# A new order for a hand-ordered two-layer transformer kernel, an earlier release of the routing banks, and ScalarE's Exp in the head attention

## What is computed

```python
xn = layernorm(x)                                    # layer 0
A  = tril(1 + s + s**2/2)                            # s = q.k/4 per head: 16 heads, feature size 16
y  = (A @ v) / rowsum(A) @ Wo.T
l  = sigmoid(xn @ gate_w) + gate_bias                # top 2 of 4 groups, then top 2 of 8 experts
f  = sum_top2 w * (silu(xn@w_gate[e]) * (xn@w_up[e])) @ w_down[e] + shared(xn)
x  = x + y + f

xn = layernorm(x)                                    # layer 1, over c (batch), t, h
p  = softmax_c((q[c,t,h] . k[c,t,h]) / sqrt(128))    # the "head attention": over the 4 batches
x1 = p[c,t,h] * sum_t v[c,t,h,:]
idx, score = top1(softmax(xn @ w_red @ norm(wg).T))
x2 = (gelu(xn @ w1[idx] + b1[idx]) @ w2[idx] + b2[idx]) * score
out = x + x1 + x2
```

## Time and profile before

| | before |
|---|---|
| median of 3 runs | 296.53 us (294.93 to 298.2) |
| the profiled execution's own time | 297.9 us |
| its span, first to last instruction | 296.2 us |
| PE busy | 261.4 us, 88% |
| DVE busy | 185.4 us, 63% |
| ACT busy | 140.2 us, 47% |
| POOL busy | 78.7 us, 27% |
| granted TensorE clock, mean | 0.954 |

### The profile page before, as it was taken

The page is one execution under the profiler, slowest core; times in us unless marked ns, Lnnn a source line. Parts: engine busy times, 40 slices in busy tenths (PEclk is TensorE's granted clock), DMA queues, the critical chain, the costliest instruction groups (busy, mean ns, idle before and its releaser), DMA issues.

```text
span 296.2 us, 6413 instructions
## 1 busy us (share of the span) xinstructions
PE 261.4 (88%) x2185; PEld 166.1 (56%) x2185; DVE 185.4 (63%) x523; ACT 140.2 (47%) x231; POOL 78.7 (27%) x113
## 2 busy tenths in 40 slices
PE   7879997899899988999999999999998719399990
PEld 5434642355553544765343945445687719299990
DVE  4759519966852477655178676768597699733330
ACT  1582724755546145434652536562633415246660
POOL 3714800100000000340030040305105160088884
PEclk9989959999999999999999999999999987789997
DMA  6890099999940000000000010002431059688930
GB/s 167 206 310 7 3 240 167 186 252 168 207 144 0 2 1 2 9 29 0 2 0 0 2 30 0 11 2 62 108 91 30 9 136 250 187 192 205 205 27 2
DMA packets 40319, 27.04 MB, mean 91 GB/s; under 512 B 5088, under 2 KB 35856, under 8 KB 40288
## 3 DMA queue, kind: packets, MB, share of 16 engines
q1 hardware_dynamic: 37024, 24.51, 37.2%
q0 software_dynamic: 3264, 2.12, 4.2%
HBM read 13.43 MB, written 13.66 MB: 91 GB/s over the span
## 4 chain that ended last, share of the span: by engine, by line
PE 62%; DVE 18%; issue 9%; POOL 4%; ACT 3%; DMA 1%; POOLq 1%; DVEq 0%; ACTq 0%
PE SC L836 12%; PE WB L809 12%; PE YT L856 11%; PE WB L896 6%; PE WB L790 4%; POOL out_dram L655 4%; PE WB L876 2%; ACT A L696 2%; PE WB L803 1%; PE WB L885 1%; PE WB L821 1%; DVE X L1203 1%; PE WB L874 1%; DVE ATT L1201 1%; PE WB L932 1%
## 5 line engine op out<-in xcount | busy, mean ns | idle before, releaser
L696 ACT ACTIVATE A<-SC 128x2048 f32<-128x2048 f32 x40 | 75.1, 1877 | 59.4 <-PE SC L836 54.1
L836 PE MATMUL SC<-QM,KT 32*128 32x512 f32 (+1 forms) x384 | 46.3, 559 | 4.5 <-ACT A L696 4.5
L856 PE MATMUL YT<-A,VH 128*18 128x256 f32 (+1 forms) x768 | 43.0, 351 | 1.5 <-DVE A L1241 1.3
L1241 DVE SCALAR_TENSOR_TENSOR A<-A,TRI 128x1024 f32<-128x1024 f32 x32 | 38.1, 1218 | 6.9 <-ACT A L696 5.5
L523 POOL TENSOR_TENSOR RSTD<-VE,NHALF 128x2 f32<-128x2 f32 (+1 forms) x12 | 10.7, 893 | 96.1 <-DVE VE L1014 96.0
L604 POOL DMA_INDIRECT xs_dram<-XN,POS x16 | 17.5, 1092 | 63.7 <-DVE POS L1118 60.6
L655 POOL DMA_INDIRECT out_dram<-KT,ROW x18 | 27.9, 1551 | 21.6 <-DVE KT L1251 16.4
L856 PEld LDWEIGHTS YT<-A,VH 128*18 128x18 f32 x768 | 19.1, 98 | 25.6 <-issue 16.8
L836 PEld LDWEIGHTS SC<-QM,KT 32*128 32x128 f32 x384 | 16.6, 183 | 21.1 <-issue 16.4
L758 ACT ACTIVATE QM<-SC,B1T 128x128 f32<-128x128 f32 x72 | 20.6, 368 | 13.0 <-PE SC L973 8.9
L809 PE MATMUL WB<-XNT,WG 128*128 128x512 f32 x40 | 23.6, 674 | 0.2 <-DVE HT L1371 0.2
(11 more groups left out here) (246 smaller groups left out, 405.3 us busy)
## 6 DMA issues: line engine op xcount, KB each, us to landing
xs_dram<-INIT SPq DMA_DIRECT2D x1, 8775.0 KB, 47.2
W1S<-in_L_ffn_w_dram SPq DMA_DIRECT2D x16, 256.0 KB
HT<-in_L_ffn_w_dram SPq DMA_DIRECT2D x7, 256.0 KB
XSL<-xs_dram SPq DMA_DIRECT2D x23, 65.0 KB
X<-_attn_hidden_states_dram SPq DMA_DIRECT2D x4, 256.0 KB, 3.4
y_dram<-INIT SPq DMA_DIRECT2D x1, 1024.0 KB, 49.5
out_dram<-X SPq DMA_DIRECT2D x4, 256.0 KB, 2.4
HT<-y_dram SPq DMA_DIRECT2D x3, 256.0 KB, 4.0
```

The source lines that it names most:

```text
L696: act.activation(squares(n).rearrange("p k r c w -> p r k (c w)"), SC[:, :, 0:k * w].rearrange("p r (k w) -> p r k w", k=k), ACT.Square, b ...
L836: last = pe.matmul(SC[:, r, cols].rearrange("p (c w) -> p c w", w=width), KT[rows, b % 2, blk, i * P:(i + 1) * P], QM[rows, b % 2, blk, 0: ...
L856: last = pe.matmul(YT[QUAD * r:QUAD * r + 2 * VW, cols], VH[:, b % 3, i, NQ * blk + r, 2 * head:2 * head + 2], squares(n)[:, k, r, head], ...
L1241: dve.scalar_tensor_tensor(out=a, in0=a, scalar=1.0, in1=keep, op0=ALU.add, op1=ALU.mult).then_inc(masked, 1)
```

## The change

1. `PLAN` is written anew: the same pieces in another order (and four new words, below). The first lines, the old and the new, and the tail are in the rows below. Each engine's order changes with it.
2. `rk`: the bank is released by the instruction that reads it last, the multiplication with the one-hot rows (rk.0, 1, 3) or the reading of the counts at the head of the table (rk.2, 4). The copy into JUNK is gone.
3. The head attention's `hc` uses ScalarE's Exp with the full scale in place of Tanh, and `hp` no longer calls `exps`. `ra`/`es` keep Tanh. The compiled program has seven loads of an activation table in place of five: one ahead of the first Exp, one ahead of the first late Gelu.
4. The first four late outputs are pieces of the plan, `fi.0` to `fi.3`. They stand behind `ha.7`, where they were, so DVE's order of them is the old one.

```diff
 PLAN = """
 ls.0 ln.0 xt.0 ls.1 q.0 k.0 ln.1 v.0 sq.0
-s.0 q.1 k.1 sq.1 mk.0 g.0 sq.2 mk.1
-s.1
+s.0 vp.0 ls.2 q.1 mk.0 k.1 g.0
+s.1 ls.3 u.0 ln.2 u.1 sq.1 g.1
...
-                    act.activation(d, d, ACT.Tanh, scale=0.5 * D ** -0.5).then_inc(diag_exped, 1)
+                    act.activation(d, d, ACT.Exp, scale=D ** -0.5).then_inc(diag_exped, 1)
...
                 ranks = w[:, 0:(hi - lo) * E1].rearrange("p (t e) -> p t e", e=E1)
-                seq(dve.tensor_tensor(q, ranks, OH[:, lo:hi], ALU.mult))
+                ins = dve.tensor_tensor(q, ranks, OH[:, lo:hi], ALU.mult)
+                if r in (ER, NR - 1):
+                    seq(ins)
+                else:
+                    used(ins, ("rk", r))
+                    wait_used(dve, ("rk", r))
...
-                seq(dve.tensor_tensor(CNTI[:], counts, EBASE[0:1], ALU.subtract))
+                used(dve.tensor_tensor(CNTI[:], counts, EBASE[0:1], ALU.subtract), ("rk", ER))
+                wait_used(dve, ("rk", ER))
...
                 dve.wait_ge(diag_exped, half + 1)
-                exps(d)
...
+            def late_slot(n):
+                for k in range(0 if n == 0 else n + IDS_AHEAD, min(n + IDS_AHEAD + 1, LATE)):
+                    keep_ids(EARLY + k)
+                finish(n)
...
-                    used(dve.tensor_copy(JUNK[:], PRI[:, 0:1]), item)
...
+                if kind == "fi":
+                    late_slot(n)
```

More of the change, by code:

```diff
@@ L55 @@
 SAVE_AT = 5
+IDS_AHEAD = 3
+PLANNED = 4
 RT_STEPS = 8
@@ new lines @@
+s.14 sq.14 oa.1 l2.0 n.2 u.8 of.1 rs.1 sq.15
+s.15 vp.2 x2.0 q.4 av.13 l2.1 av.14
+s.16 x2.1 k.5 sq.16 xd.0 pd.0 g.10 u.9 sq.17 q.5
+s.17 w.5 av.15 av.16 w.6 w.7
+s.18 u.10 xd.1 sq.18 pd.1 g.11 mk.17 g.12 u.11 ra.0
+s.19 mk.18 k.6 u.12 of.2 sq.19 es.0 mk.19 k.7 rk.0
+s.20 av.17 av.18 av.19 ys.19 sq.20 mk.20 at.2 sx.0 g.13
+s.21 sq.21 oa.2 sx.1 v.2 mk.21 n.3
+s.22 u.13 sx.2 sq.22 mk.22 rs.2 q.6 g.14
+s.23 av.20 wt.2 sq.23 sq.24 av.21 ys.22 av.22 w.8 w.9
+s.24 l2.2 u.14 g.15 u.15
+s.25 sq.25 at.3 of.3
@@ L278, in two_layers @@
         EPACK = sb("EPACK", [1, 1], I32)
-        JUNK = sb("JUNK", [P, 1])
         SPARE = sb("SPARE", [P, 1])
@@ L1404, in _ @@
                         variances(2 * n, 2 * n + 2)
-            ahead = 3
-            for s in range(EARLY, EARLY + ahead):
-                keep_ids(s)
-            for n in range(LATE):
-                if n + ahead < LATE:
-                    keep_ids(EARLY + n + ahead)
-                finish(n)
+            for n in range(PLANNED, LATE):
+                late_slot(n)
 _TURNED = {"L0_attn_Wq", "L0_attn_Wk", "L0_attn_Wv", "L0_attn_Wo", "L1_attn_Wv", "L1_ffn_w_red"}
```

75 lines of the change are left out of this document (32 added, 43 removed).

## The result

The changed kernel takes 277.38 us (median of 4 runs, 276.56 to 278.69) against 297.37 us for the kernel before, measured beside it (294.93 to 300.06). The ratio is 0.936, with an interval of 0.928 to 0.944. The direction was forecast; the size was not.

A forecast was written before the change was run, and what follows sets the result against it. PE bounds the kernel up to oa.7, then a chain through all engines. Before oa.7 2.9 + 3.2 + 2.4 + 1.6 + 0.3 = 10.4 us, plus 0.6, off 297.9 gives 286.9, as median 285.5; range 280.5 to 292.

The forecast's parts named there:

- theory W: Set up for the experiments: pieces cost the same everywhere on TensorE; the difference is small waits that no row shows.
- N: Set up for the experiments: a piece's cost on TensorE depends on its neighbours; 0.23 us per joined av pair.
- The idle time: PE's waits before oa.7 shrink by 5.8 us in all, with reserves kept for waits a queue walk does not see.
- The clock: From 14 to 24 us, without s.2's 2.09 us wait, the clock does not fall: 1.7 us; after the logits unchanged.
- The rival of a clock that stays low: Half clock from the logits to s.12, some 40 us, would give 302 us; chance 0.07, shared with a comparable stall.
- The moved pieces: eu.1, et.2, rk.3 and ed.0 go behind oa.7, under the 4.4 us before x2.7: oa.7 comes 2.9 us earlier.
- cn.0: DVE stands still about 5 us, until near 31 us, for POOL's constants; PE, in the logits, does not feel it.
- The rival of constants that end near 45 us: POOL's fills end late, routing and wt.0 shift by up to 12 us: 292 us; chance 0.24, shared with returning waits.
- Release and `fi`: Earlier release of the bank in rk.0 to rk.3, and four late outputs behind ha.7: worth nothing.
- The Exp: In the tail DVE saves 3.1 us but then waits for y_dram before sm.0: 0.6 us, between 0.0 and 0.9.
- the rival's 2.3: The Exp path gains its full 2.3 us because the early scatters land sooner: 283.8 us; chance 0.08.
- Behind oa.7: ed.4 and the reading of y_dram come no earlier after oa.7; oa.7 to ha.7 takes 30 to 31 us.

The follow-up runs named there:

- e4_apart: Changed kernel with 10 of its 18 neighbouring pairs of av pieces taken apart on TensorE alone: 277.93 us, ratio 0.944 to the kernel before.
- e7_w_full: Changed kernel with seven w pieces moved on TensorE behind the s piece that followed them: 283.35 us, ratio 0.937 to the kernel before.
- e1_order: Kernel before with nothing but the new order of the work (old release and Tanh stay): 277.83 us, ratio 0.943.
- e9_again: Changed kernel as it is, run once more on another chip: 273.39 us, ratio 0.927 to the kernel before.
- e12: Changed kernel with ha.6 ahead of sm.0 and ha.3, ha.4, ha.5 each behind its own sum: 272.50 us, ratio 0.922 to the kernel before.
- e3_pairs: Kernel before with 15 av pieces moved, on TensorE alone, each to just before the next av piece: 306.10 us, ratio 1.036.
- e6_oldhead: Changed kernel whose plan begins with the old plan up to s.8, the rest in the changed order: ratio 0.974 to the kernel before.
- e2_exp: Kernel before with nothing but the Exp in place of the Tanh: ratio 1.000.
- e11_oa_last: Changed kernel with eu.1, et.2, rk.3 and ed.0 put back ahead of oa.7: 277.70 us, ratio 0.941 to the kernel before.
- e13_junk: Changed kernel with the old release of route's bank (the copy to JUNK) put back: 278.32 us, ratio 0.939 to the kernel before.
- e10_tanh: Changed kernel with the Tanh and its three VectorE steps in place of the Exp: 273.75 us, ratio 0.927 to the kernel before.
- e15_order: Kernel before with the new order alone (old release, Tanh), on another chip: 280.46 us, ratio 0.945.

## Why the prediction was right or wrong

**The step that failed** is its first sentence on the size of the whole: "So before oa.7 at most some 16 us are not work at full speed; the rest of PE's time can only be moved." The rest was not fixed. With the changed order the same pieces took 8.4 us less on TensorE, idle time and low clock taken out. Counted over the two plans, from g.0 to oa.7 and with w taken as of the form of s, the form of the array changes 133 times before and 102 times after, mostly since 18 av pieces follow another av piece where 2 did. At 0.17 us each (e4_apart) these 31 changes are 5.3 us. The w pieces, which now stand in front of s pieces, bring some 0.7 us (1.8 at w, 1.1 lost at s; e7_w_full shows this give and take at 0.7 for seven). That leaves about 2.4 us.

An estimate from eleven of the traces gives this rest to theory W. Take for each piece the distance to the next start, and as its price the lower quartile, at full clock and without idle time, of all pieces of the same kind and size between the same forms of the array. Priced so, the new order is 5.7 us cheaper by its neighbours. What the pieces take beyond their price at full clock is 5.2 us before and 2.4 in the changed kernel: 2.8 us that no neighbour explains, most likely waits too short for the idle column or hidden under the modelled end of a row. By the same prices the ten splits of e4_apart cost 2.2 us, 0.12 for each change, so 0.17 is an upper figure. Both theories have a part, N about two thirds; no experiment took the short waits away by themselves.

The price could have been read beforehand: in the trace of the kernel before an av piece takes 1.06 us as a row wherever it stands, and its successor starts 0.99 us behind it, but 0.88 behind it when it is another av piece (0.86 to 0.88 in the changed kernel). I took durations and idle time as the two parts of PE's time, and never the distance from start to start.

**The idle time.** Forecast 5.8 us, trace 8.1. The first stretch went as forecast (2.09 to 0.21; kept 0.6). From 44 to 120 us I kept 0.4 and half of 3.14 for what a walk through the queues does not see, and there was nothing: both stretches are without a gap. Keeping reserves of 2.0 us was the smaller error. From 120 us on I expected no gain, and the 2.10 us there include 1.8 us (0.45 and 1.38) around a late squaring (ScalarE's stall, last section) that e1, e4, e9 and e12 do not have.

**The clock.** I tied the low clock of the first stretch to the 2.09 us wait of s.2. e3_pairs and e6_oldhead have the same head and the same wait, and the clock is 1.00 from 14 to 24 us in both; e2_exp shows 0.83 as the earlier trace rows. So the fall comes in some executions and not in others, and my reason for 1.7 us of gain was wrong. After the logits the low clock was shorter than before in the changed kernel (1.8 us and not 3.4), and in e9_again it did not come at all. The rival of a clock that stays low did not show in any of these runs.

**The moved pieces.** Forecast 2.9; 3.3 in the trace before, 3.2 in e11_oa_last, 4.3 at the end there. (The 3.5 of that run's expectation also holds what the other pieces of these kinds lost.) Right in mechanism. I left out et.2 and the waits that the squeezed pieces would have had.

**cn.0.** Right: VectorE stands still for 6.15 us until 32.66 (forecast about 5, until near 31), and PE works through the logits meanwhile:

```profile
32.66 0.14 DVE L1296 TENSOR_SCALAR WGNORM<-WGNORM 8x1 f32<-8x1 f32 x1 [6.15 <-POOL WGNORM L599]
```

The rival of constants that end near 45 us fell.

**Release and `fi`.** Forecast nothing; 0.3 us in e13_junk. Right in size there, but by luck: I argued that ed.2 "has moved behind" and that the wait had no follower. e1_order shows it in full, with ed.2, the early scatters and the reading behind it.

**The Exp.** The mechanism was right (the wait for y_dram takes over), and the size on one chip: 0.3 to 0.4 us in e10_tanh, forecast 0.6, nothing in e2_exp. Between e15_order and e13_junk it is 2.1 us (1.6 by the distances), near the rival's 2.3. With the Tanh sm.0 starts without a wait in both pairs (e10_tanh, e15_order). With the Exp VectorE is 3.1 us ahead and waits for y_dram, 1.69 + 0.99 us in e9_again and 0.99 + 0.53 in e13_junk: what is left, 0.4 and 1.6, is what the distances show. How much the Exp brings hangs on when the reading lands, and that differs between chips by more than the term. My bounds of 0.0 and 0.9 also took the earlier trace rows wrongly: 3.3, 4.0 and 4.2 us are the times of the reading's three parts, issued one behind the other, and not a spread of the first. The two loads take 1.28 us each, and the Exp starts at 219.16, 0.01 us behind the end of the load. The Trainium skill's 1.38 us of draining for each load ("ScalarE: Activation LUTs", "What ACT_TABLE_LOAD costs") does not show as a gap on either side: the Gelu ahead ends at 217.85 and the load starts at 217.87.

**Behind oa.7.** I wrote that ed.4 comes no earlier behind oa.7 than before. It comes later: eu.4 waits 2.42 us for the Gelu of eu.3, and the reading of y_dram is issued 22.1 us behind oa.7, not 20.1. That is why the distance was 32.3 and not 30.4. In e9_again, without ScalarE's stall, it is 31.3, with the reading at 20.2; so about 1 us of the miss goes with the stall. The other 0.9 is in part the second wait for y_dram (0.99 us), for a part of the reading that I had not looked at; how it divides with the third early output behind the table was not tried. x2.7 follows oa.7 by 4.3 us, as forecast, and the scatters stand 1.88 us apart.

**The range.** It had 6.5 us above the forecast and 5 below. All my rivals but one took something away; the only one on the fast side was the Exp, 1.7 us. The lower bound was not the bound of anything: I had kept 5.4 us of idle time and 3.4 of low clock, and with both gone my own sum gives 285.5 - 8.8 = 276.7.

## What to carry to other kernels

On TensorE read the time from start to start, by kind of the next piece, not the rows' durations: pieces that use another part of the array (here `128*18`, `32*128`, `128*128`) cost 0.12 to 0.17 us at each change, and an order that puts like beside like gains without removing any wait. But a piece that fills the time of another engine's step (here 2.1 us beside each squaring) can only be moved if something else fills it, and a better head is worth nothing when the rest cannot use it: try such orders whole. When a walk through the queues finds no wait, give the range a case in which it is right everywhere.
